# Context and token projections of a two-layer gated transformer block as one phase

## The reference, cut to what matters

```python
# layer 0: x (2, 1024, 512), ctx (2, 2048, 256)
h = layernorm(x)
q, k, v = h @ Wq + bq, h @ Wk + bk, h @ Wv + bv
qc      = h @ Wcq + bcq
kc, vc  = ctx @ Wck + bck, ctx @ Wcv + bcv
x = x + tanh(g_xattn[0]) * ((attend(q, k, v, causal) + attend(qc, kc, vc)) @ Wp + bp)
x = x + tanh(g_ffn[0]) * experts0(layernorm(x))
# layer 1
q1      = layernorm(x) @ Wq1 + bq1
k1, v1  = ctx @ Wk1 + bk1, ctx @ Wv1 + bv1
x = x + tanh(g_xattn[1]) * (attend(q1, k1, v1) @ Wo + bo)
x = x + tanh(g_ffn[1]) * experts1(layernorm(x))
```

## Time and profile before

| | us |
|---|---|
| median of 3 runs (lowest, highest) | 4030.9 (4030.63, 4036.47) |
| the profiled execution | 4039.2 |
| its span | 4037.5 |
| mean granted clock of PE in it | 0.953 |
| busy in the span: PE | 3698.3 (92%) |
| DVE | 2506.9 (62%) |
| ACT | 2060.4 (51%) |
| POOL | 1770.6 (44%) |

### The profile page before, as it was taken

The page is one execution under the profiler, slowest core; times in us unless marked ns, Lnnn a source line. Parts: engine busy times, 40 slices in busy tenths (PEclk is TensorE's granted clock), DMA queues, the critical chain, the costliest instruction groups (busy, mean ns, idle before and its releaser), DMA issues. The chain is left out here.

```text
span 4037.5 us, 76143 instructions
## 1 busy us (share of the span) xinstructions
PE 3698.3 (92%) x30244; PEld 2594.3 (64%) x30244; DVE 2506.9 (62%) x2873; ACT 2060.4 (51%) x3649; POOL 1770.6 (44%) x874
## 2 busy tenths in 40 slices
PE   6989699999999998869996699999998859999998
PEld 5768456666665664459995355555554548888886
DVE  4345687878888784666664677777773553333342
ACT  2222266666666665146662366666665144444432
POOL 0000287687778777002110488888886011111110
PEclk9999799999999999879998799999999869999999
DMA  4478724424442431636653522222211423333341
GB/s 160 166 235 296 203 77 104 109 74 105 98 114 59 110 87 45 227 118 201 219 186 115 148 78 79 75 80 78 76 44 55 174 87 117 117 117 108 115 113 38
DMA packets 290266, 485.13 MB, mean 120 GB/s; under 512 B 23104, under 2 KB 121408, under 8 KB 287936
## 3 DMA queue, kind: packets, MB, share of 16 engines
q1 hardware_dynamic: 274368, 443.01, 36.5%
q0 software_dynamic: 14080, 37.76, 4.1%
q10 hardware_dynamic: 1536, 0.40, 0.1%
HBM read 350.67 MB, written 130.02 MB: 119 GB/s over the span
## 5 line engine op out<-in xcount | busy, mean ns | idle before, releaser
L803 ACT ACTIVATE attn_probs<-attn_low 128x512 f32<-128x512 f32 (+1 forms) x2368 | 1234.6, 595 | 467.4 <-PE attn_low L714 351.7
L844 DVE TENSOR_REDUCE attn_parts<-attn_mx 128x4 f32<-128x2048 f32 x538 | 1232.8, 2291 | 366.3 <-PE attn_mx L686 365.6
L665 POOL TENSOR_TENSOR attn_psums<-attn_psums,attn_probs 128x1024 f32<-128x1024 f32 x536 | 1275.1, 2379 | 66.6 <-ACT attn_probs L803 1.4
L714 PE MATMUL attn_low<-attn_queries,attn_keys 97*128 97x256 f32 (+1 forms) x4736 | 914.7, 311 | 13.5 <-ACT attn_probs L803 5.5
L714 PEld LDWEIGHTS attn_low<-attn_queries,attn_keys 97*128 97x128 f32 x4736 | 658.3, 190 | 371.7 <-ACT attn_probs L803 187.7
L731 PE MATMUL attn_low<-attn_probs,attn_values 128*32 128x256 f32 x9472 | 629.4, 383 | 1.4 <-ACT attn_probs L803 1.4
L1528 DVE TENSOR_TENSOR ring_low<-ring_raw,ring_high 128x2048 fp32r<-128x2048 f32 x128 | 293.1, 2292 | 206.7 <-ACT ring_high L1485 206.7
L662 POOL TENSOR_TENSOR attn_psums<-attn_probs 128x1024 f32<-128x1024 f32 x88 | 209.6, 2382 | 371.6 <-ACT attn_probs L803 371.6
L731 PEld LDWEIGHTS attn_low<-attn_probs,attn_values 128*32 128x32 f32 x9472 | 247.6, 109 | 182.8 <-issue 2.1
L1442 PE MATMUL ffn_up<-ffn_xH,ring_high 128*128 128x256 f32 (+1 forms) x1024 | 351.0, 343 | 2.7 <-DVE ffn_xL L1534 2.7
L1442 PE MATMUL ffn_up<-ffn_xH,ring_low 128*128 128x256 f32 (+1 forms) x1024 | 348.2, 340 | 0.0
(11 more groups left out here) (200 smaller groups left out, 4434.6 us busy)
## 6 DMA issues: line engine op xcount, KB each, us to landing
ring_raw<-in_L_ffn_W_dram SPq DMA_DIRECT2D x128, 1024.0 KB, 5.5
attn_keys<-l_cross_keys SPq DMA_DIRECT2D x96, 512.0 KB, 6.9
attn_queries<-l_queries SPq DMA_DIRECT2D x48, 512.0 KB, 4.8
l_cross_keys<-projc_high SPq DMA_DIRECT2D x64, 256.0 KB, 2.2
l_cross_keys<-projc_lowp SPq DMA_DIRECT2D x64, 256.0 KB, 2.4
l_cross_values<-projc_vout SPq DMA_DIRECT2D x64, 256.0 KB, 2.5
attn_keysn<-l_cross_keys SPq DMA_DIRECT2D x16, 1024.0 KB, 5.0
attn_values<-l_cross_values SPq DMA_DIRECT2D x32, 512.0 KB, 8.3
```

What stands on the lines that cost most here:

```text
L665: pool.tensor_tensor(ps, ps, at, ALU.add).then_inc(added, 1)
L714: mm = pe.matmul(out[:, n0:], KS[b][0:3 * HD + 1, h, kb * P:(kb + 1) * P], QS[b][0:3 * HD + 1, h, job.qb * QB + n0:(job.qb + 1) * QB], sta ...
L803: act.activation(probs[:, m % RING, i // 2, heads, n0:], sc[:, item % SC, :].rearrange("p (h q) -> p h q", q=QB)[:, :, n0:], ACT.Exp, scal ...
L844: op = dve.tensor_reduce(into, seen, AX.X, ALU.max)
```

## The change

The projections of layer 0's tokens and of the context for both layers become one phase.

- `Source` describes one input with its weights, and `Blocks` the order in which blocks of the sources come: 0, 1, 0, 0, 1, 0, 0, 1, 0, 0, 1, 0, with 0 the context and 1 the tokens. In the context's blocks, row and column units alternate; in the tokens' they don't.
- All loops over blocks are written out.
- The first block is a context block. Its load, four context weights and all eight biases are issued by SP inside the constants stage, behind the gates (`st.begin`).
- The other weights are loaded by POOL between the blocks' loads, as room in `raw` comes free. They are split at given units: two context weights ahead of the first turn, two at units 3 and 4 of block 0, the token weights at unit 12 of block 0 and units 1, 4 and 8 of block 1.
- Tokens are normalized in place. In the combined phase there is one input buffer, so the load of a block is issued when the block before has been turned. In blocks with 16 units, the next block is measured at unit 3 and normalized at unit 5; its turn stays at unit 8.
- Rows and columns have rings and store semaphores of their own.
- Layer 1's projection runs the same code with two input buffers; SP issues its first block ahead of the weight, and POOL the second block at once.

```diff
@@ constants
+def set_constants(nc, c, g_xattn, g_ffn, st, early):
...
                 sp.dma_start(c["gates"][:, 0:2], g_xattn.partition_broadcast(P)).then_inc(loaded, DMA)
                 sp.dma_start(c["gates"][:, 2:4], g_ffn.partition_broadcast(P)).then_inc(loaded, DMA)
+                st.begin(sp, early)
@@ class Source
+        if mixed:
+            half = len(self.outs) // 2
+            self.units = [(n, t) for r in range(half) for t in range(4) for n in (r, half + r)]
+        else:
+            self.units = [(n, t) for n in range(len(self.outs)) for t in range(4)]
@@ class Projections
+    def begin(self, sp, early):
+
+        self.load_x(sp, 0, self.first_in)
+        for w in early:
+            self.load_weight(sp, w)
+        for w in self.weights:
+            self.load_bias(sp, w)
@@ project
+    def norm_at(g):
+        return (3, 5) if len(sources[plan.at[g][0]].units) > 4 else (0, 0)
+
+    def turn_at(g):
+        return max(len(sources[plan.at[g][0]].units) // 2, 3)
...
+            def load_weights(g):
+                while waiting and splits[waiting[0]][0] <= g:
+                    w = waiting.pop(0)
+                    if held[w]:
+                        pool.wait_ge(w_low, max(rank[x] for x in held[w]) + 1)
+                    st.load_weight(pool, w)
+
+            for g in range(1, G):
+                if g >= st.slots:
+                    pool.wait_ge(turned, plan.chunks[g - st.slots + 1])
+                st.load_x(pool, g, st.x_in[g % st.slots])
+                load_weights(g)
...
+            def turn_tokens(g):
+                s, slot = plan.at[g][0], g % st.slots
+                if sources[s].norm:
+                    pe.wait_ge(normed, plan.norms[g + 1])
...
+                for ch in range(sources[s].C):
+                    n = plan.chunks[g] + ch
+                    if n >= 2:
+                        pe.wait_ge(xT_ready, n - 1)
...
+            turn_tokens(0)
+            for g, (s, _, _) in enumerate(plan.at):
+                C = sources[s].C
+                pe.wait_ge(xT_ready, plan.chunks[g + 1])
+                for k, (n, t) in enumerate(sources[s].units):
+                    if k == turn_at(g) and g + 1 < G:
+                        turn_tokens(g + 1)
+                    u = plan.units[g] + k
+                    pe.wait_ge(w_low, rank[s, n] + 1)
+                    if u >= RING:
+                        pe.wait_ge(evacuated, u - RING + 1)
...
+            deviation(0)
+            for w in split_at(-1, 0):
+                split(w)
+            turned_high(0)
+            for s in range(len(sources)):
+                act.wait_ge(st.bias_in[s], DMA * len(sources[s].outs))
+            for g, (s, _, _) in enumerate(plan.at):
+                for k, (n, t) in enumerate(sources[s].units):
+                    if k == norm_at(g)[0] and g + 1 < G:
+                        deviation(g + 1)
+                    if k == turn_at(g) and g + 1 < G:
+                        turned_high(g + 1)
+                    for w in split_at(g, k):
+                        split(w)
...
+                    if r >= RING:
+                        act.wait_ge(row_out[r % RING], 2 * DMA * (r // RING))
...
+                    if k == norm_at(g)[0] and g + 1 < G:
+                        measure(g + 1)
+                    if k == norm_at(g)[1] and g + 1 < G:
+                        normalize(g + 1)
+                    if k == turn_at(g) and g + 1 < G:
+                        turned_low(g + 1)
+                    for w in split_at(g, k):
+                        split(w)
@@ program
+            st = Projections(nc, ph, c, "proj", [context, tokens], [0, 1, 0, 0, 1, 0, 0, 1, 0, 0, 1, 0], 1)
+            early = [(0, 0), (0, 2), (0, 1), (0, 3)]
+            set_constants(nc, c, g_xattn, g_ffn, st, early)
+            project(nc, ph, c, st, {(0, 0): (-1, 0), (0, 2): (-1, 0), (0, 1): (0, 3), (0, 3): (0, 4), (1, 0): (0, 12),
+                                    (1, 1): (1, 1), (1, 2): (1, 4), (1, 3): (1, 8)}, early, True)
...
-        project(nc, "proj1", c, x1, T, D, True, [(L1_xattn_Wq, L1_xattn_bq, l1_queries)], [])
+        with Phase(nc, "proj1") as ph:
+            tokens = Source(x1, T, D, True, [(L1_xattn_Wq, L1_xattn_bq, l1_queries)], [], False)
+            st = Projections(nc, ph, c, "proj1", [tokens], [0, 0, 0, 0], 2)
+            project(nc, ph, c, st, {(0, 0): (-1, 0)}, [(0, 0)], False)
```

More of the change, by code:

```diff
@@ L75, in sem, with constants @@
         return self.sems[-1]
-def constants(nc, keep, g_xattn, g_ffn):
+def constants(keep):
     c = {"keep": keep}
@@ L86, in constants @@
         c[name] = keep.sb(name, shape, dtype)
+    return c
+def set_constants(nc, c, g_xattn, g_ffn, st, early):
     with Phase(nc, "const") as ph:
@@ new lines, with __init__ @@
+class Source:
+    def __init__(self, src, tokens, width, norm, rows_out, cols_out, mixed):
+        self.src, self.tokens, self.width, self.norm = src, tokens, width, norm
+        self.outs = [(w, bias, dst, True) for w, bias, dst in rows_out] + [(w, bias, dst, False) for w, bias, dst in cols_out]
+        self.C = width // P
+        if mixed:
[3 more added lines that the diff above has]
+            self.units = [(n, t) for n in range(len(self.outs)) for t in range(4)]
+        self.blocks = [(b, j) for b in range(B) for j in range(tokens // BLK)]
@@ new lines, with __init__ @@
+class Blocks:
+    def __init__(self, sources, order):
+        nexts = [0] * len(sources)
+        self.at = []
+        for s in order:
+            self.at.append((s,) + sources[s].blocks[nexts[s]])
+            nexts[s] += 1
+        self.units, self.chunks, self.norms = [0], [0], [0]
+        for s, _, _ in self.at:
+            self.units.append(self.units[-1] + len(sources[s].units))
+            self.chunks.append(self.chunks[-1] + sources[s].C)
+            self.norms.append(self.norms[-1] + sources[s].norm)
+        self.rows, self.cols, rows, cols = {}, {}, 0, 0
+        for g, (s, _, _) in enumerate(self.at):
+            for k, (n, _) in enumerate(sources[s].units):
+                if sources[s].outs[n][3]:
+                    self.rows[g, k], rows = rows, rows + 1
+                else:
+                    self.cols[g, k], cols = cols, cols + 1
+        self.n_rows, self.n_cols = rows, cols
@@ L1596, in program @@
     with Phase(nc, "keep") as keep:
-        c = constants(nc, keep, g_xattn, g_ffn)
+        c = constants(keep)
         logits = keep.sb("logits", [P, NTILE, E])
@@ L1600, in program @@
         weight = [keep.sb(f"weight{n}", [P, E, k // P]) for n, k in enumerate((k0, k1))]
-        project(nc, "proj0", c, x, T, D, True,
-                [(L0_xattn_Wq, L0_xattn_bq, queries), (L0_xattn_Wk, L0_xattn_bk, keys),
-                 (L0_xattn_Wcq, L0_xattn_bcq, cross_queries)], [(L0_xattn_Wv, L0_xattn_bv, values)])
-        project(nc, "projc", c, ctx, TC, CC, False,
-                [(L0_xattn_Wck, L0_xattn_bck, cross_keys), (L1_xattn_Wk, L1_xattn_bk, l1_keys)],
-                [(L0_xattn_Wcv, L0_xattn_bcv, cross_values), (L1_xattn_Wv, L1_xattn_bv, l1_values)])
+        with Phase(nc, "proj") as ph:
+            context = Source(ctx, TC, CC, False,
+                             [(L0_xattn_Wck, L0_xattn_bck, cross_keys), (L1_xattn_Wk, L1_xattn_bk, l1_keys)],
+                             [(L0_xattn_Wcv, L0_xattn_bcv, cross_values), (L1_xattn_Wv, L1_xattn_bv, l1_values)], True)
+            tokens = Source(x, T, D, True,
+                            [(L0_xattn_Wq, L0_xattn_bq, queries), (L0_xattn_Wk, L0_xattn_bk, keys),
+                             (L0_xattn_Wcq, L0_xattn_bcq, cross_queries)], [(L0_xattn_Wv, L0_xattn_bv, values)], False)
+            st = Projections(nc, ph, c, "proj", [context, tokens], [0, 1, 0, 0, 1, 0, 0, 1, 0, 0, 1, 0], 1)
[3 more added lines that the diff above has]
+                                    (1, 1): (1, 1), (1, 2): (1, 4), (1, 3): (1, 8)}, early, True)
         attention(nc, "attn0", c,
```

409 lines of the change are left out of this document (194 added, 215 removed).

## The result

Over four executions each, the median went from 4031.57 us (4030.63 to 4036.47) to 4005.92 us (4000.16 to 4008.12). The ratio is 0.9926, 95% interval 0.9914 to 0.9938. That is 25.7 us gained; the forecast was 24.4 us and 4006.5.

What follows compares the result with a forecast made beforehand. PE was taken to bound the context stage, with losses at the start, seam and turns. The phase's 21.3 us plus layer 1's 3.1 gave 24.4, taking the median from 4030.9 to 4006.5; range 3991 to 4020, chance 0.8.

Steps and rivals of the forecast that it cites:

- The seam and the edges: Between token and context stages: 14.9 us of store wait, barriers, loads and splits go entirely; edges give 25.3 us in all.
- The first product: At the start: SP's issues hold the barrier until 12, then 5.1 us; first product at 17.1 instead of 27.54.
- My rival that early loads don't start PE early: At the start: barrier waits for SP's issues and slow bias pieces; first product at 24, total 4013; chance 0.06.
- Block 0's lump: First block: DVE's two weight splits pile onto token normalizing; the turn costs 9.0 us, plus 1.8 of slow products behind it.
- The later turns: Three later token turns inside context blocks cost PE 5.55 us each, bounds 3.3 and 8.9.
- The walk: DVE's work through a later token turn: PE waits 1.45 us for normalizing, 1.75 for xL, and resumes at 16.75.
- the rival that put the total at 4021: Stops at turns slow PE's clock: 1.8 us at three more turns, 8 us a turn, SP held to 13; chance 0.17.
- the 396.2: Combined phase from first product to last evacuation: 189.3 + 179.5 + 9.0 + 1.8 + 3 x 5.55 us.
- Edits at nothing: Unrolled loops (bounds +2 and -2), separate semaphores and alternating rows and columns, POOL's queue and in-place normalizing priced at nothing.
- My rival of stores at every turn (4088): All 11 turns meet store waits, 8.9 + 1.8 us each, +82 us; chance of ending above 4039: 0.03.
- Layer 1: Layer 1's projection: tokens by SP ahead of the weight come 3.0 us earlier, later blocks 0.1; 3.1 us in all.
- The sharing of two queues: Rival: layer 1's first two token loads share evenly, the first landing about 2.7 us later; total 4009; chance 0.05.

Runs made afterwards that it cites:

- two-phase run: Changed kernel split into two phases, all context blocks then tokens, four biases ahead of the barrier; attention's first memset at 418.6 us, against 414.91 in the changed kernel.
- contexts first: Changed kernel, one phase, with all eight context blocks ahead of the four token blocks; attention's first memset at 404.5 us, against 414.91.
- two contexts first: Changed kernel with block order context, context, token, four times, token weights split one block later; attention's first memset at 411.5 us, against 414.91.
- rows first: Changed kernel with context blocks' eight row units, then eight column units, instead of alternating; attention's first memset at 426.5 us, time 4024.48 us.
- the run with the edit in layer 1: Changed kernel with POOL issuing layer 1's second token block only after SP's weight landed; layer 1's first product 17.17 us after its stage's first issue, against 19.45.
- statistics sooner: Changed kernel with next token block measured at unit 1, normalized at unit 3, except in the first block; attention's first memset at 410.05 us, against 414.91.
- all together: Changed kernel with contexts ahead of tokens, token biases later, earlier statistics, layer 1's weight before its second token block; median 3990.91 us, ratio 0.989 to the kernel before.

## Why the prediction was right, step by step

| step | predicted | measured |
|---|---|---|
| SP's last issue ends | 10.9 | 11.97 |
| first product | 17.1 | 17.53 |
| block 0, from the first product to unit 8 | 21.9 | 21.68 |
| slow products behind that stop | 1.8 | 0 |
| each later token turn | 5.55 | 5.14, 4.53, 4.52 |
| slow products behind the later turns | 0 | 0.9, behind the first |
| first product to the start of the last evacuation | 396.2 | 391.6 |
| first attention load | 418 | 414.8 |
| layer 1 | 3.1 | 2.1 |
| median gained | 24.4 | 25.7 |

**The seam and the edges** were right in kind and size: with the seam removed nothing took its place. The two-phase run puts it at 17.3 us in the new code, for the 14.9 of the prediction.

**The first product** was right for the reason given: SP's issues hold the barrier, with two stalls. That it was right to 0.4 us is in part luck: 10.9 was the middle between two bounds, 1.1 too early, and the 5.1 us from the barrier to F measured 4.7. My rival that early loads don't start PE early asked for a first product at 24. It named the right mechanism at the wrong price: the early issue buys nothing (the run without it has F 2.6 us sooner and A 0.5 later, which is no difference), but the loads behind the barrier don't cost 24 either.

**Block 0's lump** was right to 0.2 us. Its slow products were in another place. I put 1.8 us behind the stop at unit 8. PE had stood for 1.99 us ahead of unit 7, and there the window shows 0.69 of clock and 6 matmuls in 3 us; the time they lost lay beside the normalizing that the turn waited for anyway. Behind 39.21 products came 0.23 apart. What I had wrong is the place of the stop: I let unit 7 start "2.2 late" and priced only what came behind unit 8. The two waits at unit 8 were 1.31 and 0.56 us.

**The later turns** are a term that was mis-sized: 5.55 each for 5.14, 4.53 and 4.52, 2.5 us in all. The walk has the right stops in the right order, put down to normalizing and xL, but 1.06 and 1.36 long, not 1.45 and 1.75. I added DVE's passes by their durations. Back to back they start sooner than that:

```profile
229.60 0.69 DVE L471 TENSOR_TENSOR proj_vout<-proj_bank,proj_bias 128x512 f32<-128x512 f32 x1
...
230.20 0.74 DVE L463 SCALAR_TENSOR_TENSOR proj_lowp<-proj_bank,proj_bias,proj_high 128x512 fp32r<-128x512 f32 x1
...
230.86 0.68 DVE L471 TENSOR_TENSOR proj_vout<-proj_bank,proj_bias 128x512 f32<-128x512 f32 x1
231.46 0.68 DVE L434 TENSOR_TENSOR proj_xL<-proj_turn,proj_xH 128x512 fp32r<-128x512 f32 x1
```

The starts are 0.60, 0.66 and 0.60 apart where the durations are 0.69, 0.74 and 0.68. The record's durations overlap by 0.08, so a chain of seven is half a microsecond shorter than their sum. In the walk this makes each of the two waits 0.4 us shorter; another 0.3 is the last transposes, 1.01 us (232.19 to 233.20) for my 1.3.

**The clock** fell at one of the three later turns, so the rival that put the total at 4021 came true in part. At the first of them the stops of 1.06 and 1.36 us were followed by a granted clock of 0.63 and 0.51; it cost 0.6 us in the transposes and 0.9 behind them. At the other two the same stops weren't followed by it. I had it at no turn, the rival at all three with 1.8 each.

**The phase was 4.6 us shorter** than the 396.2. The slow products behind block 0 that didn't come make 1.8, block 0 itself 0.2 and the later turns 2.5, and 0.9 were lost to the slow products behind one of them: 3.6 in all. The last 1.0 is what is left of three errors that I didn't see. The stages of the kernel before hold three stops of PE that I took for work, 1.02 and 1.12 us in the token stage (41.44 and 48.31) and 1.58 in the context stage, all on DVE's `lowp`. With the slow restarts they make 4.2 us inside the 179.5 and 189.3:

```profile
254.63 0.50 PE L264 MATMUL projc_bank<-projc_xH,projc_wH 128*128 128x512 f32 x1 [1.58 <-DVE projc_lowp L361]
```

So "inside the context stage PE is the bound" holds but for this stop. The kernel after has no such stops but the one in block 0. Against the 4.2 stand 1.3 us, since I took 1.8 for each of the token stage's three slow stretches where they cost 1.7, 1.2 and 1.2, and 2.0 us because at full clock the matmuls of the kernel after start 0.2337 us apart in the mean where those of before start 0.2324 apart; the cause of that is open. That these three nearly cancel is luck. The phase began 0.4 us later than said and so ended 4.1 before my 413.3.

**The barrier at the end** took 0.9 us more than before. I had it unchanged. In the four runs whose phase ends on a token block it took 3.84 to 3.86, in the six that end on a context block with alternating units (the kernel after among them) 4.60 to 5.05, and 3.85 in the run that ends on a context block with its column units last. So it isn't the context block but the alternation that costs 0.8 to 1.2 us here. That it leaves more stores under way at the end, since a row unit stores twice as much, is an argument, not shown.

**Edits at nothing.** Unrolling: right, 0.4 us. Alternation and separate rings "can only lessen the store waits": right in sign, but priced at nothing, as if the old order would have done as well here. It wouldn't: without it the phase is 11.6 us longer. My rival of stores at every turn (4088) had the mechanism, and what kept store waits away was this edit: without it ACT and DVE waited some 25 us for stores in all. **Biases** cost nothing at unit 0, as said: its evacuation starts at 20.58 on PE's product.

**Layer 1** is the step whose mechanism was wrong. The tokens came 3.2 us sooner (3.0 said). But "the weight follows some 3 us later, when ACT is ready for it" left out that POOL's second block, 1 MB issued 0.5 us after the first, shares the engines with it: 10.7 us instead of 7.8. The run that holds this load back has the weight after 7.8 us and the first product 2.3 us sooner. Two errors of opposite sign, 3.2 us too little in the phase and 1.0 too much in layer 1, left the total close: that forecast and measured gain are only 1.3 us apart is in part luck.

**The sharing of two queues.** The row speaks against even sharing: SP's first tokens took 5.5 us with POOL's 1 MB beside them and 5.4 without. The Trainium skill (DMA: Bandwidth & Descriptors, Queues, rings and completion order) lets each DMA engine go round-robin between queues, packet by packet; by that rule the first load would have been slower by most of POOL's. The trace doesn't agree for the first load. For the second it might: the weight lost 2.9 us. Which rule decides isn't shown.

## What to carry to other kernels

A gain of one edge is only kept if nothing behind it waits for what was moved: biases moved behind a barrier gave 5.1 us at the start and kept 2.1, moved with their wait they gave 3.2 and kept 3.35. When phases are merged, look for lumps: walk the busiest helper engine through one turn, since its average load (19.4 of 22.4 us by the prediction's sum) hides waits, and a shift by two units took 1.5 us off each turn. Look for stops inside the old stages too, before they are taken over as work. And where a change both reorders the work and alternates kinds of stores, price each of them against the new order, not the old one.

## What the runs showed of the hardware

- SP stood longer at some issues while loads were under way: 2.48 and 1.68 us for bias loads, against 0.43 to 0.69 for most others, and up to 2.66 in the run with the biases behind the barrier.
- Products stay slow after PE's start for a varying time, while the record gives a clock of 1.00. With first products at 17.50, 17.53, 17.60 and 17.57 us (contexts first, the kernel after, two contexts first, rows first), the first 7, 10, 12 and 14 steps from one matmul to the next were long, nearly all 0.43 us. A step of 0.43 us rather than 0.23 is what 1.2 GHz makes against 2.4. At about 0.2 us each this moves a stretch by up to 1.4 us, so edits worth less than that need more than one execution. The Trainium skill (TensorE: Matmul & The Clock Gate, Part 1: The HAM clock gate) says the same, that the count of slow matmuls varies between runs of one kernel. The trace agrees: with the same code up to A, it was 10 in the kernel after and 13 in the run with the edit in layer 1.
- In block 0, a stop of 1.99 us was followed by slow products, and here the record does show it (0.69). The same two stops of 1.06 and 1.36 us at a turn stand nineteen times in the traces of the kernel after and six of its variants. Six times slow products followed, once in each of six kernels, and thirteen times none did. So the stops' length alone didn't decide it. None came behind the thirteen turns of the variants whose only stop was 0.98 or 1.29 us (statistics sooner, contexts first, two phases, all together), and in the run with rows first they came behind all four turns.
